# Two attention layers and two mixtures of experts on a graph: destinations spread from transposed ones, routing shared out over four engines, ranks by maxima, and four reorderings

## What is computed

```python
# 1: graph attention, 4 heads of 64
h = (x @ W).reshape(N, 4, 64)
e = leaky_relu(a_src[src] + a_dst[dst], 0.2); e = exp(e - segment_max(e, dst)[dst])
out = segment_sum(e / segment_sum(e, dst)[dst] * h[src], dst) + bias
# 2: six experts, the best two for each node
logits = softmax(relu(x @ router_w1 + b1) @ router_w2 + b2)
top_w, top_i = top_k(logits, 2); weights = softmax(top_w)
out = sum of the two experts' three-layer networks, weighted
# 3: graph attention, 1 head of 256, with the edges' attributes in the score
# 4: eight experts, all of them for every node, weighted by a softmax
```

## Time and profile before

| | us |
|---|---|
| three runs | 4315.14, 4308.82, 4315.09 (median 4315.09) |
| the profiled execution | 4308.81 |
| its span in the trace | 4307.1 |
| PE busy (share of the span) | 3250.0 (75%) |
| DVE busy | 2923.0 (68%) |
| POOL busy | 2021.3 (47%) |
| ACT busy | 1554.4 (36%) |
| mean granted TensorE clock, as a share of full speed | 0.818 |

### The profile page before, as it was taken

How to read it: one execution, slowest core, us unless ns; L and a number is a source line. 1 busy time by engine, 2 the same in 40 slices (tenths; PEclk the granted TensorE clock), 3 DMA queues, 4 the chain that set the end, 5 groups by cost and what they waited for, 6 DMA issues and landing times. The chain is left out here.

```text
span 4307.1 us, 73738 instructions
## 1 busy us (share of the span) xinstructions
PE 3250.0 (75%) x15898; PEld 2470.8 (57%) x15898; DVE 2923.0 (68%) x9596; ACT 1554.4 (36%) x4357; POOL 2021.3 (47%) x2122
## 2 busy tenths in 40 slices
PE   6466666676766789964566666666668999999999
PEld 4244444444444578853344444444447888888888
DVE  5599999999997867655566666666657765454554
ACT  3233333333332224432333333333323333434343
POOL 3777777777770034446777777777740000000000
PEclk9577777777776579987677777777779999999999
DMA  5444444444464146744444444444452000000000
GB/s 147 102 109 108 108 106 106 106 107 107 106 98 89 39 108 191 190 128 123 108 108 108 108 109 108 108 108 108 108 64 76 6 8 5 7 5 7 5 7 8
DMA packets 379249, 372.18 MB, mean 86 GB/s; under 512 B 246016, under 2 KB 305580, under 8 KB 378634
## 3 DMA queue, kind: packets, MB, share of 16 engines
q0 software_dynamic: 99072, 273.04, 25.7%
q1 hardware_dynamic: 277994, 94.55, 10.0%
q10 hardware_dynamic: 1818, 0.74, 0.1%
HBM read 326.48 MB, written 41.60 MB: 85 GB/s over the span
## 5 line engine op out<-in xcount | busy, mean ns | idle before, releaser
L782 POOL DMA_INDIRECT g_G<-rows,g_pack x1856 | 1754.9, 946 | 627.7 <-issue 497.2
L815 PE MATMUL bank<-g_G,g_MB 128*125 128x260 f32 x1856 | 670.6, 509 | 248.0 <-DVE acc L1023 246.7
L1023 DVE SCALAR_TENSOR_TENSOR acc<-acc,g_c,bank 125x65 f32 (+1 forms) x2320 | 617.4, 315 | 134.9 <-DVE acc L1023 67.2
L815 PEld LDWEIGHTS bank<-g_G,g_MB 128*125 128x125 f32 x1856 | 426.7, 248 | 392.0 <-DVE acc L1023 284.2
L815 PE MATMUL bank<-g_G,g_M 128*125 128x257 f32 x1856 | 631.2, 487 | 20.5 <-DVE acc L1023 20.3
L1321 ACT ACTIVATE e_h<-bank,bn_shift,bn_scale 128x250 f32<-128x250 f32 x800 | 400.6, 555 | 531.5 <-PE bank L1274 411.1
L886 ACT ACTIVATE g_mt_d<-bank,unode 125x256 bf16<-125x256 f32 x928 | 380.9, 460 | 437.1 <-PE bank L800 436.9
L815 PEld LDWEIGHTS bank<-g_G,g_M 128*125 128x125 f32 x1856 | 417.1, 241 | 145.8 <-DVE acc L1023 25.6
L1445 DVE SCALAR_TENSOR_TENSOR X<-bank,e_cw,X 125x256 f32 (+1 forms) x400 | 175.1, 479 | 408.4 <-PE bank L1283 406.4
L1283 PE MATMUL bank<-e_w,e_h 128*125 128x256 f32 x1400 | 334.0, 382 | 20.5 <-ACT e_h L1321 16.3
L898 ACT ACTIVATE g_MT<-g_mt_d,ones 125x512 bf16<-125x512 bf16 x464 | 335.0, 722 | 11.4
(11 more groups left out here) (326 smaller groups left out, 4539.6 us busy)
## 6 DMA issues: line engine op xcount, KB each, us to landing
g_G<-rows,g_pack POOLq DMA_INDIRECT x1856
acc<-in_edge_attr SPq DMA_DIRECT2D x50, 476.0 KB
g_pack<-edge_pack SPq DMA_DIRECT2D x928, 2.0 KB
g_drow<-edge_dst SPq DMA_DIRECT2D x928, 1.0 KB
expert_out<-x_y SPq DMA_DIRECT2D x54, 256.0 KB
g_qe<-edge_q SPq DMA_DIRECT2D x464, 1.0 KB
rows<-acc SPq DMA_DIRECT2D x25, 227.5 KB
rows<-n_T SPq DMA_DIRECT2D x25, 224.9 KB
```

What stands on the lines that cost most here:

```text
L782: nc.gpsimd.indirect_dma_start(G[:, r, q, :], None, rows_d[l], bass.IndirectOffsetOnAxis(ap=pack[:, r, q, 0:1], axis=0)).then_inc(S(p + f" ...
L815: mm_ = nc.tensor.matmul(sum_bank(r, k, u)[0:TN, 0:HW], left, G[:, rk, q, :], start=(c == 0), stop=(c == C - 1))
L1023: ins = nc.vector.scalar_tensor_tensor(at, at, c1[:, rk, u, h:h + 1], sum_bank(r, k, u)[0:TN, h * W:(h + 1) * W], ALU.mult, ALU.add)
```

## The change

It does the following.

- **attention**: `edge_dst`, `drow` and its loads go. LT is copied once more as bfloat16 (`LTb`, on ACT, behind LT), and `spread` multiplies LTb by a matrix with ones in one row (`pick_row`, a column of the identity, broadcast), four matmuls of 128 columns in the place of one of 512. `place` becomes one activation with `minus_n` (minus the partition's number) as bias. The scan waits for LTb, since it overwrites LT.
- **rows(0)**: `lo_i`, `hl` and `unode` go; the slot with the last load of X stands ahead of the tables' transfers.
- **route**: SP waits for the router's weights before it loads the experts'. The second tile's `y` is made by ACT (four activations), the addition to X is POOL's, `y` has four buffers; `xn` comes a slot later, and PE's order within a slot becomes transposes, first matrix, second matrix.
- **sort**: the two best experts are found by maxima over tensors of 125 x 300. Places are marked four rows at a time in bfloat16: DVE makes `is_hi` and `hot_lo`, ACT weighs `is_hi` by the node's number in its tile and by the tile's number (three activations), PE multiplies both halves at once (216 columns), and the buffers are doubled. The table of tiles is made behind the loop and not ahead of it.
- **dense_experts**: `finish(1)` and `root(1)` stand ahead of the first `normal_shares`, and the first group's `weigh` stands ahead of the `relu` that it followed.

```diff
+                        slot(NG - 5, (NG - 5) % 4, (NG - 5) // 4)
...
+                        for i in range(NG - 4, NG + 2):
                             slot(i, i % 4, i // 4)
...
-                                if u % 2 == 0 and late(i, 2):
-                                    after(sp, p + "spread", i * V - 2 * V + (v_ + 1))
-                                    held(sp, p + "spread_seen")
-                                sp.dma_start(drow[:, u, :], dst_d[:, bass.ds(s, UE)]).then_inc(S(p + f"drow_in{(r - 1) % RING}"), 16)
...
+                                pe.wait_ge(S(p + "LTb"), i)
...
-                            nc.tensor.matmul(bank[2 + v_ % 2][0:TN, :], ones_bf[:, :], drow[:, 2 * v_:2 * v_ + 2, :].rearrange("k u e -> k (u e)"),
-                                             start=True, stop=True).then_inc(S(p + "spread"), 1)
+                            for k in range(CP):
+                                row = (v_ * CP + k) * H
+                                mm_ = nc.tensor.matmul(bank[2 + v_ % 2][0:TN, k * P:(k + 1) * P], pick_row[:, row:row + 1].broadcast_to([QH, TN]), LTb[:, :],
+                                                       start=True, stop=True)
+                            mm_.then_inc(S(p + "spread"), 1)
...
                                 after(act, p + "MT", i * V - V + (v_ - 1))
-                            for k in range(2):
-                                ins = nc.scalar.activation(mt_d[:, v_ % 2, k * C:(k + 1) * C, :],
-                                                           bank[2 + v_ % 2][0:TN, k * UE:(k + 1) * UE].rearrange("p (e c) -> p c e", c=C), ACT.Abs,
-                                                           bias=unode[0:TN, bass.ds(i * U - U + (2 * v_ + k), 1)])
...
+                                                 bias=minus_n[0:TN, :]).then_inc(S(p + "mt_abs"), 1)
 
...
+                            if late(i, 2):
+                                act.wait_ge(S(p + "spread"), i * V - V)
+                            act.wait_ge(S(p + "LT"), i)
+                            nc.scalar.copy(LTb[:, :], LT[:, :]).then_inc(S(p + "LTb"), 1)
...
+                            v.wait_ge(S(p + "LTb"), i)
...
-                            relu(0, i, i * NX + e, e)
                             if isinstance(i, int) and i == 0 and e == 1:
                                 weigh(0)
+                            relu(0, i, i * NX + e, e)
                             if follows(i):
...
                             add_bias(i, r, e)
                             if follows(i):
                                 if e == 1:
-                                    if isinstance(i, int) and i == 0:
-                                        finish(1)
-                                        root(1, FIRST)
                                     normal(i + 1)
...
+                    finish(1)
+                    root(1, FIRST)
                     normal_shares(0, 0)
...
+                    sp.wait_ge(S(p + "w"), 16 * 6)
...
+                            pool.wait_ge(S(p + "y_act"), i + 1)
+                            held(pool, p + "y_seen")
+                            xt = X[:, bass.ds(i * GT, GT), :]
+                            nc.gpsimd.tensor_tensor(xt, xt, y[:, r, :, :], ALU.add).then_inc(S(p + "x"), 1)
+                    run(pool, slot)
...
                         r1, r2 = (r - 1) % 2, r % 2
+                        if grouped(i, 0):
+                            if late(i, 4):
+                                act.wait_ge(S(p + "x"), i - 3)
...
+                            for h in range(H):
+                                k = i * GT + GT - 1
+                                ins = nc.scalar.activation(y[:, r, GT - 1, h * DH:(h + 1) * DH], acc[:, bass.ds(k * HW + h * W, DH)], ACT.Copy, scale=den[:, bass.ds(k * H + h, 1)])
+                            ins.then_inc(S(p + "y_act"), 1)
+                        if grouped(i, 1):
+                            act.wait_ge(S(p + "ag"), i * GT)
+                            nc.scalar.activation(sd[:, (r - 1) % 4, :], ag[:, (r - 1) % 4, :, 1], ACT.Sqrt, bias=eps_ln[0:TN, :]).then_inc(S(p + "sd"), 1)
...
+                            v.wait_ge(S(p + "sd"), i - 1)
+                            nc.vector.reciprocal(rs[:, r2, :], sd[:, r2, :]).then_inc(S(p + "rs"), 1)
                         if grouped(i, 0):
...
+                            for u in range(GT - 1):
                                 k = i * GT + u
...
-                            v.wait_ge(S(p + "sd"), i)
...
-                            nc.vector.tensor_tensor(xt, xt, y[:, r % 2, :, :], ALU.add).then_inc(S(p + "x"), 1)
...
+                    def weigh(h, r):
+                        act.wait_ge(S(p + "is_hi"), h + 1)
+                        if late(h, 2):
...
+                        nc.scalar.activation(hot_hi[:, r, :, 0, :], is_hi[:, r, :, :], ACT.Copy, scale=nid[0:TN, 0:1])
+                        for k in range(2):
+                            ins = nc.scalar.activation(hot_hi[:, r, 2 * k:2 * k + 2, 1, :], is_hi[:, r, 2 * k:2 * k + 2, :], ACT.Copy, scale=tid[:, bass.ds(h * 2 + k, 1)])
+                        ins.then_inc(S(p + "hot"), 1)
...
+                            mm = nc.tensor.matmul(bank[2][:, 0:2 * HI], hot_lo[:, r, k, :], hot_hi[:, r, k, :, :].rearrange("p z n -> p (z n)"), start=(first_ and k == 0), stop=(last_ and k == 3))
+                        mm.then_inc(S(p + "placed"), 1)
...
-                    one_, other = ex[:, :, :].unsqueeze(3).broadcast_to([TN, NT, NX, NX]), ex[:, :, :].unsqueeze(2).broadcast_to([TN, NT, NX, NX])
-                    nc.vector.tensor_tensor(gt[:, :, :, :], other, one_, ALU.is_gt)
...
+                    def first_best(from_, out):
+                        step(nc.vector.tensor_tensor(code[:, :, :], from_, wide(top[:, :]), ALU.is_equal))
+                        step(nc.vector.tensor_tensor(code[:, :, :], code[:, :, :], early[:, :].unsqueeze(1).broadcast_to([TN, NT, NX]), ALU.mult))
+                        step(nc.vector.tensor_reduce(top[:, :], code[:, :, :], AX.X, ALU.max))
+                        step(nc.vector.tensor_tensor(out, code[:, :, :], wide(top[:, :]), ALU.is_equal))
+
+                    first_best(ex[:, :, :], pick[:, 0, :, :])
+                    step(nc.vector.scalar_tensor_tensor(rest[:, :, :], pick[:, 0, :, :], -2.0, ex[:, :, :], ALU.mult, ALU.add))
+                    step(nc.vector.tensor_reduce(top[:, :], rest[:, :, :], AX.X, ALU.max))
+                    first_best(rest[:, :, :], pick[:, 1, :, :])
...
+                    def mark(h, r):
+                        if late(h, 2):
+                            v.wait_ge(S(p + "hot"), h - 1)
+                            v.wait_ge(S(p + "placed"), h - 1)
+                        held(v, p + "placed_seen")
+                        nc.vector.tensor_tensor(is_hi[:, r, :, :], iota_b[0:TN, 0:HI].unsqueeze(1).broadcast_to([TN, 4, HI]),
+                                                hi[:, bass.ds(h * 4, 4)].unsqueeze(2).broadcast_to([TN, 4, HI]), ALU.is_equal).then_inc(S(p + "is_hi"), 1)
+                        nc.vector.tensor_tensor(hot_lo[:, r, :, :], iota_b[0:TN, :].unsqueeze(1).broadcast_to([TN, 4, P]),
+                                                lo[:, bass.ds(h * 4, 4)].unsqueeze(2).broadcast_to([TN, 4, P]), ALU.is_equal).then_inc(S(p + "hot_lo"), 1)
+                    halves(v, mark)
...
-                    def mark(h, ready):
-                        for k in range(4):
-                            t, j = h * 2 + k // 2, h * 4 + k
-                            if ready:
-                                v.wait_ge(S(p + "placed"), h * 4 + (k - 3))
-                                held(v, p + "placed_seen")
-                            nc.vector.tensor_scalar(hot_lo[:, k, :], iota_b[0:TN, :], lo[:, bass.ds(j, 1)], None, ALU.is_equal)
```

237 lines of the change are left out of this document (110 added, 127 removed).

## The result

| | before | changed |
|---|---|---|
| median of the runs, us | 4313.27 (4 runs, 4308.82 to 4315.14) | 4264.08 (4 runs, 4262.32 to 4267.06) |
| ratio, 95% interval | 1 | 0.9886 [0.9874, 0.9898] |
| profiled execution, span | 4308.81, 4307.1 | 4263.31, 4261.5 |
| mean granted clock | 0.818 | 0.833 |

What follows compares the result with a forecast made beforehand. Bounds: POOL's gathers and DVE in attention, PE or DVE in route, DVE in sort. Terms -6.6 + 0 - 5.4 - 19.6 - 5.2 = -36.8 against 4308.8 give 4272; half the median's 6.3 offset makes 4275, range 4250 to 4294.

Steps and rivals of the forecast that it cites:

- make 1.65: Sort's loop: ACT's 1.48 us and a wait of 0.15 to 0.2 give 1.65 us a set, saving 13.2 us.
- -2.1: rows(0), slot 3: removing `lo_i` and the two conversions to `hl` from DVE saves 2.1 us.
- -4.5: End of rows(0): the last X is issued six microseconds earlier, so DVE's wait of 4.48 us for it goes.
- -5.2: dense_experts' start: `finish(1)` and `root(1)` fit into DVE's idle time, ending PE's stall and low clock, saving 5.2 us.
- the period is PE's: 3.5 against 3.65: Route: at a 1.2 GHz clock PE sets a group's time, 3.5 us for 3.65, saving 3.6 over 24 groups.
- PE's work per group does not change: Route: PE is busy 3.63 and 3.53 us a group at clock 0.50, and the change leaves that work alone.
- 3.0 us less: Route's start: holding back the experts' weights shortens the 7.89 us wait for the router's weights by 3.0 us.
- 928 loads by SP, which does nothing else that is late: Attention: removing these loads gains nothing, since SP is not late; the attention stages were forecast at 0.
- The exclusion of POOL and DVE: Rival, 13%: in route POOL's add and DVE's `y` block each other, +1 in place of -5.4, total 4281.
- DVE's other instructions read one tensor: Route: reason for keeping -5.4 although POOL's add can block DVE's `y`, which has two SBUF inputs.
- The rising clock: Rival, 22%: denser PE lifts route's clock to 2.4 GHz, period about 2.75, route -25, total 4255; if intermittent, 4265.
- ACT did not bind sort: Rival, 10%: ACT's three activations take 2.2 us a set, sort's loop stays at 55 us, total 4288.

Runs made afterwards that it cites:

- the ring of three: The changed kernel with three buffers for hot_lo, is_hi and hot_hi in sort: 4255.77 us, ratio 0.986.
- the old orders: The changed kernel with PE's and ACT's parts of a route slot back in their old order: 4266.29 us, ratio 0.9893.

## Why the prediction was right, and which sizes were off

- **The sign and the order of size** held: -45.6 us in the span for -36.8, and the largest term, sort, was within 1.1 us. The 8.8 us beyond the forecast are 4.8 in route and 7.9 in the stages for which I had forecast nothing, less 3.9 by which rows(0), sort and dense_experts gave less than forecast. That 4264 lies inside the range owes something to its width: of those 7.9 us only some 3 have a cause that the runs show.
- **Sort** held in both steps. The ranks took 5.9 us as worked out. A set took 1.705 for "make 1.65": the wait that I had added without a mechanism is the chain through two buffers, and the ring of three shows it.
- **rows(0)**: "-2.1" came as worked out. Of "-4.5" for X the profile gives 3.1, since DVE still stands 1.39 us there for the square root on ACT.
- **dense_experts**: "-5.2" held (4.2 to 5.7). The -3.3 of the two profiles mixes in a clock that fell earlier in one of them.
- **Route** came to -10.2 for -5.4, and three terms make it by the group starts: 5.6 less at the first group (15.7 to 10.1), 5.8 less over 24 periods (88.3 to 82.5), 1.2 more behind the last (8.3 to 9.5).
- **Route, "the period is PE's: 3.5 against 3.65"** was mis-sized, 3.71 to 3.43, and its two steps failed. "As long as the clock stays at 1.2 GHz the period is PE's" was read from PE's busy time, which hid waits: before the change PE's transposes waited for DVE's `xn` and its first matrix for ACT's copy. "PE's work per group does not change" failed too: the old orders take 3.53 at the least that a run shows, the new one 3.25. By the runs, without the addition and half of `y` DVE lets go 0.16 (3.71 to 3.55 in the old orders), and the new orders give 0.12 on top (3.55 to 3.43), where DVE's `xn` binds again. The stand of 3.24 us behind the stores of `xn` took back a part; of that wait I had nothing.
- **Route, "3.0 us less" at the start**: up to the 19th group the wait is worth 3.7, namely 5.5 at the first group less what its own queue costs at the fifth. "+1.2" for the deeper pipeline was right.
- **Attention, "928 loads by SP, which does nothing else that is late"**: this step failed. SP was not late, but with its small transfers DVE waited longer for POOL's gathered rows. It is worth some 3 us in attention(1).
- **The rivals.** The exclusion of POOL and DVE happened, at about the price that I gave (0.42 in the mean and 0.95 at most, for "up to 0.85"), and didn't eat the gain: DVE with it is still ahead of where it was. "DVE's other instructions read one tensor" was no shelter: with one input `y` stood as well, and the one `xn` of the changed kernel's route that ran beside POOL's addition from its start took 0.93 us for 0.40. The rising clock is real in a way that I had only half: it comes for ten to some tens of microseconds, never for the whole stage, and moves the same code's route between 99.1 and 102.1 us. In the changed kernel's profile it came while the first groups passed (0.63 and 0.71 in the second and third stretch of 10 us), where the filling of the pipeline and the stores bound, and gave nothing. ACT did not bind sort (it does with three buffers, at 1.28 us a set and not 2.2), MT was not late in attention(0), and each part did what it says.

What stays open: the -4.0 us of attention(0) and the -1.7 of picked_experts and rows(1) have no cause shown, and are about as large as what the same code varies by. Nor is it shown how much of DVE's lateness in route comes from its standing behind POOL, since `y` with one input stood too, nor what makes the clock rise there.

## What to carry to other kernels

A PE that is busy throughout is not yet the bound: compare the start of each of its parts with the end of what it needs, since a start that follows by the same 0.05 us in group after group is a wait. Its busy time is not a floor either, since the order of its instructions sets how much of a weight load is covered (0.14 us a group here). Engines that work in order and feed each other need orders that agree, or each round pays for it (4.76 against 3.55 us here). A ring of two buffers over three engines was a chain; a third buffer took 10 us out of a loop of 44. Where a clock comes and goes, compare the starts of the same groups in stretches of one clock, not the lengths of stages: two of the experiments here read wrongly by their totals.

## What the runs showed of the hardware that was not expected

- A DVE instruction with two inputs in SBUF and POOL's addition exclude each other so regularly that a mean shows it: 842 ns for 425, over 25 groups. One with a single input took 710 in the mean and 290 where the addition wasn't beside it. A single case, POOL and DVE of the changed kernel:

```profile
1360.25 1.27 POOL L1535 TENSOR_TENSOR X<-X,r_y 125x512 f32<-125x512 f32 x1 [2.82 <-ACT r_y L1591]
...
1360.43 1.37 DVE L1629 TENSOR_TENSOR r_y<-acc,r_den 125x256 f32<-125x256 f32 x1
```

DVE's ends 0.28 us after POOL's does, and POOL's is not longer than the 1.26 that it takes elsewhere: the one that came second stood.
- With 928 loads of 1 KB on SP's queue, a small part of the bytes, DVE waited 5.4 us longer for gathered rows at one place (14.81 for 9.44 us), while the steady iterations kept their 20.01 us.
- The same matmuls at the same clock take 3.53 or 3.25 us a group: 0.14 us by their order, the rest by waits for ACT that PE's busy time does not show.
- The clock at a place that no edit touches differs between kernels: the second row of matmuls in dense_experts took 1.96 us in six kernels, the one before among them, and 3.50 to 3.70 in the changed kernel and six others. Such a difference of 1.6 us must be taken out before an edit there is judged.
